# Edge rows placed in source order by plain scatters, and the edge sum of a four-layer graph network taken on TensorE without accumulating scatters

## What is computed

```python
def _L3_gnn_ref(x, edge_index, edge_attr, u, batch, W1, b1, W2, b2, Wa, ba, Wb, bb):
    row, col = (edge_index[0], edge_index[1])
    h = jnp.concatenate([x[col], edge_attr], axis=1)
    h = jax.nn.relu(h @ W1.T + b1)
    h = jax.nn.relu(h @ W2.T + b2)
    summed = jax.ops.segment_sum(h, row, num_segments=n)
    ...
    agg = summed / jnp.maximum(cnt, 1.0)[:, None]
    z = jnp.concatenate([x, agg, u[batch]], axis=1)
    z = jax.nn.relu(z @ Wa.T + ba)
    return z @ Wb.T + bb
```

## Time and profile before

| what | value |
|---|---|
| median of 3 runs | 4369.33 us (4359.36 to 4374.9) |
| the profiled execution | 4391.7 us, its span 4390.0 us |
| PE busy | 2941.5 us (67%) |
| DVE busy | 2594.5 us (59%) |
| POOL busy | 2417.1 us (55%) |
| ACT busy | 1475.1 us (34%) |
| TensorE's granted clock, mean | 0.728 of full speed |
| DMA | 338.20 MB, 77 GB/s on average |

### The profile page before, as it was taken

One profiled execution on the slowest core, in us unless ns is written; L12 is line 12 of the kernel. 1 busy time (PEld: TensorE's weight loads), 2 busy tenths in 40 slices (PEclk: granted clock), 3 DMA queues, 4 the chain that ended last, 5 costly groups with the idle time before them and its releaser, 6 DMA issues. The chain is left out here.

```text
span 4390.0 us, 76379 instructions
## 1 busy us (share of the span) xinstructions
PE 2941.5 (67%) x16134; PEld 2027.4 (46%) x16135; DVE 2594.5 (59%) x9305; ACT 1475.1 (34%) x3181; POOL 2417.1 (55%) x1836
## 2 busy tenths in 40 slices
PE   1636666666666666656567785887878878778762
PEld 0324544444444454443232332666656666666541
DVE  6148888888888887776954443444344443444422
ACT  0124444444444444443010000443333333333320
POOL 0056666666666666550000000588888888888881
PEclk9955555555555555556778876888988989899876
DMA  1353333333333333782603230455555555555543
GB/s 43 100 125 98 97 95 102 97 97 108 90 97 97 106 98 89 86 103 98 169 25 86 71 93 4 47 54 54 53 54 53 54 54 53 54 54 53 54 43 74
DMA packets 654307, 338.20 MB, mean 77 GB/s; under 512 B 437168, under 2 KB 614627, under 8 KB 653284
## 3 DMA queue, kind: packets, MB, share of 16 engines
q0 software_dynamic: 148736, 86.57, 20.5%
q1 hardware_dynamic: 487814, 143.62, 15.5%
q10 hardware_dynamic: 17568, 106.20, 6.0%
HBM read 158.05 MB, written 202.84 MB: 82 GB/s over the span
## 5 line engine op out<-in xcount | busy, mean ns | idle before, releaser
L1847 POOL DMA_INDIRECT sums<-el_rows,el_idx x816 | 1269.2, 1555 | 782.2 <-DVE el_rows L2061 533.9
L828 POOL DMA_INDIRECT at_hs<-table,at_rec_s x976 | 1140.3, 1168 | 614.9 <-DVE at_hw L1122 310.3
L966 PE MATMUL near_ps<-at_pair_hot,at_src_low_hot 128*128 128x425 f16 x976 | 507.4, 520 | 580.1 <-ACT at_count_s L864 319.8
L864 ACT CAST at_count_s<-near_ps 128x400 f16<-128x400 f32 x976 | 481.9, 494 | 987.5 <-PE near_ps L966 446.0
L2059 DVE CAST el_idx<-el_place 128x4 uint32<-128x4 f32 x204 | 35.3, 173 | 840.6 <-DMA sums<-el_rows,el_idx 791.8
L938 PEld LDWEIGHTS sums_ps<-at_hw,at_hit 128*128 128x128 f32 x1952 | 472.9, 334 | 36.3 <-issue 31.7
L966 PEld LDWEIGHTS near_ps<-at_pair_hot,at_src_low_hot 128*128 128x128 f16 x976 | 135.4, 139 | 722.8 <-ACT at_count_s L864 397.9
L938 PE MATMUL sums_ps<-at_hw,at_hit 128*128 128x66 f32 x1952 | 442.2, 408 | 8.7 <-DVE acc L1012 8.7
L1409 PE MATMUL sum_total<-chunk,sum_parts 128*128 128x512 f16 (+1 forms) x700 | 264.2, 391 | 119.9 <-DVE chunk L1511 98.3
L1004 DVE TENSOR_SCALAR at_pair_hot<-iota_wide,at_rec_s 128x400 f16<-128x400 f16 x976 | 324.7, 335 | 0.0
L1995 ACT ACTIVATE el_h<-el_h_ps,el_valid 128x128 f32<-128x128 f32 x816 | 232.6, 368 | 239.3 <-PE el_h_ps L1909 175.8
(11 more groups left out here) (339 smaller groups left out, 5095.2 us busy)
## 6 DMA issues: line engine op xcount, KB each, us to landing
slots<-at_count_s ACTq DMA_DIRECT2D x122, 850.0 KB
chunk<-slots SPq DMA_DIRECT2D x480, 100.0 KB
el_rec<-attr SPq DMA_DIRECT2D x816, 32.0 KB
attr<-in_edge_attr SPq DMA_DIRECT2D x19, 1248.0 KB
at_rec_s<-meta SPq DMA_DIRECT2D x992, 3.5 KB
at_hs<-table,at_rec_s POOLq DMA_INDIRECT x976
el_pair<-meta SPq DMA_DIRECT2D x816, 1.0 KB
sums<-el_rows,el_idx POOLq DMA_INDIRECT x816
```

The costliest lines, as they stand in the source:

```text
L828: pool.indirect_dma_start(hs[:, s, u, :], None, k.table, bass.IndirectOffsetOnAxis(rec[:, s, u, 0:1].bitcast(U32), 0)).then_inc(gathered[s ...
L864: a.copy(count[:, (n.o + d) % 2, i, 0:AW], near[:, (n.o + d) % 2, 0:AW]).then_inc(count_ready, 1)
L966: pe.matmul(near[:, s, 0:SW], low_hot[:, s, i, :], pair_hot[:, s, i, :], start=False, stop=True, skip_group_check=(i > 0)).then_inc(near_r ...
L1847: pool.indirect_dma_start(k.sums_flat[a], bass.IndirectOffsetOnAxis(idx[:, j, a:a + 1], 0), rows[:, j, a, :], None, compute_op=ALU.add).th ...
```

## The change

- A new stage `edge_places` counts, for each of the 25 tiles of source nodes, the edges before each edge (VectorE's scans, sums over partitions on TensorE), and writes for every edge its end node, its source and its place in the order of source tiles (`edge_ends`). It also makes the visits of the edge loop, now for tiles of source nodes; the second pass of `schedule` goes.
- All 782 columns of edge rows (64 features, the end node and the source: 66 words) are scattered to their places in `edge_rows`, one indirect DMA of 128 rows per column. 244 of them (two a step) are in attention, behind the step's 8 gathers; the other 538 are in blocks of 17 (the last has 11) in the stages from ln0 to edge_tables: 1 in ln0, 6 in the first neighbour sum, 1 in the degree layer, 1 in ln1, 5 in each further neighbour sum, 1 in each linear layer, 1 in ln2, and 4 (62 columns) in edge_tables. Three buffers hold a piece or a block. The copy into `attr` and the zeroing go.
- The edge loop, again 102 visits of 8 tiles, loads edge rows of one tile of source nodes, and POOL gathers the end nodes' rows of x beside them (816 gathers). TensorE turns both together, one product with K = 128 takes the place of y and the mask, and the sum over sources is a product with a one-hot matrix of the source within its tile (`hot`). VectorE adds the result to `edge_sum` in SBUF, at a tile read from a table.
- `node_update` takes `edge_sum` as it is. The tables y in edge_tables go; x is written to HBM there (`node_rows`).

```diff
+PIECE = 2
+PARTS = 3
+BLOCK = 17
+
+NB3 = -(-(EC + NT) // (3 * B)) * 3
+LATER = EC - PIECE * NB0
+SIZES = [min(BLOCK, LATER - b) for b in range(0, LATER, BLOCK)]
...
+def edge_places(nc, k):
+
+    with Stage(nc) as c:
...
+            pe.wait_ge(count_ready, 1)
+            pe.matmul(before[:, 0:NT], k.below[:], count[:], start=True, stop=True)
+            pe.matmul(column[:, 0:NT], k.ones_f[:], count[:], start=True, stop=True).then_inc(counted, 1)
+            for t in range(NT):
+                pe.wait_ge(value_ready, t + 1)
+                for i in range(2):
+                    m = pe.matmul(place[:, i, 0:W], k.ident[:], value[:, t % 3, i * W:(i + 1) * W], start=(t == 0),
+                                  stop=(t == NT - 1))
+                m.then_inc(value_added, 1)
...
+            for t in range(NT):
+                v.tensor_scalar(mask[:, t], k.tile_h[:], float(t), None, ALU.is_equal).then_inc(run_ready, 1)
+                if t:
+                    dve.wait_ge(run_ready, 2 * t)
+                    v.tensor_tensor_scan(run[:, t - 1], mask[:, t - 1], none[:], 0.0, ALU.add, ALU.add).then_inc(run_ready, 1)
...
+            for t in range(NT):
+                if t >= 3:
+                    dve.wait_ge(value_added, t - 2)
+                v.scalar_tensor_tensor(value[:, t % 3], run[:, t], base[:, t:t + 1], mask[:, t], ALU.add, ALU.mult
+                                       ).then_inc(value_ready, 1)
...
+            dve.wait_ge(value_added, NT)
+            for i in range(2):
+                v.tensor_copy(k.row_ends[:, i * W:(i + 1) * W, 2].bitcast(U32), place[:, i, 0:W]).then_inc(place_ready, 1)
...
+            def piece(n, d):
+
+                s = (n.o + d) % PARTS
+                if n.after(PARTS - d):
+                    sp.wait_ge(part_placed[s], n.thirds(d) * (16 * PIECE))
+                    sp.sem_inc(passed, 1)
+                sp.dma_start(part[:, s, :, 0:D], features[:, bass.ds(n(PIECE, d * PIECE), PIECE), :]).then_inc(part_loaded[s], 16)
+                sp.dma_start(part[:, s, :, D:ER + 1], row_ends[:, bass.ds(n(PIECE, d * PIECE), PIECE), :]
+                             ).then_inc(part_loaded[s], 16)
...
-            for a in range(NACC):
-                for i in range(8):
-                    sp.dma_start(k.sums_flat[a].rearrange("(p r) h -> p (r h)", p=P)[:, i * ZW:(i + 1) * ZW],
-                                 k.zero[:]).then_inc(sums_zeroed, 16)
...
+                s = n.o % PARTS
+                pool.wait_ge(part_loaded[s], n.thirds(0) * 32 + 32)
+                pool.sem_inc(passed, 1)
+                for i in range(PIECE):
+                    pool.indirect_dma_start(k.edges, bass.IndirectOffsetOnAxis(part[:, s, i, ER:ER + 1].bitcast(U32), 0),
+                                            part[:, s, i, 0:ER], None).then_inc(part_placed[s], 16)
...
+def place_blocks(nc, k, pool, blocks):
+
+    for b in blocks:
+        s = b % PARTS
+        pool.wait_ge(k.block_loaded[s], 32 * (b // PARTS + 1))
+        for i in range(SIZES[b]):
+            pool.indirect_dma_start(k.edges, bass.IndirectOffsetOnAxis(k.block_rows[:, s, i, ER:ER + 1].bitcast(U32), 0),
+                                    k.block_rows[:, s, i, 0:ER], None).then_inc(k.block_placed[s], 16)
...
+                for b, after in zip(blocks, due_after):
+                    if after == i < DC - 1:
+                        load_block(nc, k, act, b + PARTS)
...
+                    pool.wait_ge(loaded[s], it * (16 * B) + 16 * B)
                     pool.sem_inc(passed, 1)
-                    for a in range(NACC):
-                        if not (first and j == 0):
-
-                            pool.wait_ge(added[a], it * 64 + 16 * j)
-                            pool.sem_inc(passed, 1)
-                        pool.indirect_dma_start(k.sums_flat[a], bass.IndirectOffsetOnAxis(idx[:, j, a:a + 1], 0),
-                                                rows[:, j, a, :], None, compute_op=ALU.add).then_inc(added[a], 16)
-            body(0, True)
+                    for u in range(B):
+                        pool.indirect_dma_start(edge[:, s, u, 0:D], None, k.nodes,
+                                                bass.IndirectOffsetOnAxis(edge[:, s, u, 2 * D:2 * D + 1].bitcast(U32), 0)
+                                                ).then_inc(gathered[s][u // 4], 16)
...
+                    t = pe.transpose(z_ps[:, j % 2, u * P:(u + 1) * P], edge[:, s, 4 * h + u, 0:2 * D], k.ident[:])
+                t.then_inc(turned, 1)
...
+                pe.matmul(h1_ps[:, j % 2, :], k.w1[:], z_t[:, j % 2, :], start=True, stop=True).then_inc(h1_ready, 1)
...
+                v.tensor_tensor(hot[:, j % 2], own[:, s, 4 * h:4 * h + 4].unsqueeze(2).to_broadcast([P, 4, P]),
+                                k.iota_row[:].unsqueeze(1).to_broadcast([P, 4, P]), ALU.is_equal).then_inc(hot_ready, 1)
...
+            def adds(q, j, m, first):
+                tiles = tiles_of(m, j % 2)
                 dve.wait_ge(sum_ready, q + 1)
-                dve.wait_ge(join_ready, n1)
-                if done is not None:
-                    for a in range(NACC):
-                        dve.wait_ge(added[a], done)
-                ch(v.tensor_copy(idx[:, j], place[:, s, 4 * h:4 * h + 4]))
-                ch.wait()
-                v.tensor_copy(rows[:, j].rearrange("p u h -> p (u h)"), sum_ps[:, j % 2, :]).then_inc(rows_ready, 1)
+                for u in range(4):
+                    to = k.part[:, bass.ds(tiles[u], 1), :].rearrange("p t h -> p (t h)")
+                    if u or not first:
+                        dve.wait_ge(added, q * 4 + u)
+                    v.tensor_tensor(to, to, sum_ps[:, j % 2, u * P:(u + 1) * P], ALU.add).then_inc(added, 1)
...
+            layernorm(nc, k, "ln0", x_t=k.x_t, ahead=range(AHEAD), blocks=blocks(1))
+            neighbour_sum(nc, k, 0, range(DC), blocks(6))
+            degree_layer(nc, k, blocks(1))
+            layernorm(nc, k, "ln1", x_t=k.x_t, blocks=blocks(1))
             keep(nc, k)
...
+                neighbour_sum(nc, k, i + 1, range(DC) if i % 2 else range(DC - 1, -1, -1), blocks(5))
+                linear_layer(nc, k, i, blocks(1))
+            layernorm(nc, k, "ln2", x_t=k.x_t, blocks=blocks(1))
...
+            edge_tables(nc, k, blocks(len(SIZES)))
             edge_loop(nc, k)
-        node_update(nc, k)
```

More of the change, by code:

```diff
@@ L1454, in _ @@
                 pe.sem_inc(skipped, 1)
+        @block.gpsimd
+        def _(pool):
+            place_blocks(nc, k, pool, blocks)
+        due_after = [-(-(i + 1) * DC // len(blocks)) - 1 for i in range(len(blocks))]
         @block.scalar
@@ L1480, in _ @@
             act.wait_ge(copied, DC)
+            for b, after in zip(blocks, due_after):
+                if after == DC - 1:
+                    load_block(nc, k, act, b + PARTS)
         @block.vector
@@ L2162, in _ @@
             step(v.reciprocal(share[:], share[:]))
-            dve.wait_ge(loaded, 16 * NACC)
-            for a in range(1, NACC):
-                step(v.tensor_tensor(part[:, 0], part[:, 0], part[:, a], ALU.add))
-            v.tensor_tensor(part[:, 0], part[:, 0], share[:].unsqueeze(2).to_broadcast([P, NT, H]),
+            v.tensor_tensor(mean[:], k.part[:, 0:NT], share[:].unsqueeze(2).to_broadcast([P, NT, H]),
                             ALU.mult).then_inc(mean_ready, 1)
@@ L2255, in gnn_stack_kernel @@
                 group_records(nc, k)
+                edge_places(nc, k)
             with ExitStack() as c1:
```

586 lines of the change are left out of this document (283 added, 303 removed).

## The result

| | median | runs |
|---|---|---|
| kernel before | 4372.11 us | 4 (4359.36 to 4379.41) |
| changed kernel | 5139.16 us | 4 (5129.51 to 5172.04) |

The ratio is 1.177 (95% interval 1.171 to 1.183). The prediction said 4105 us, 4020 to 4290; the kernel became 767 us slower, 1034 us above the forecast. The profiled execution has a span of 5127.8 us.

The account below looks back on a forecast made before the run. POOL's queue was taken to bound the edge loop, with its 816 accumulating scatters. The terms 116 + 48 + 98 - 495 - 31 gave -264 us, a median of 4105 us, range 4020 to 4290.

Parts of the forecast that it names:

- edge_places: New stage with nothing beside it: 123 us, less 7 for schedule's tile pass, so +116, between +90 and +160.
- ln0 to ln2: Middle stages before edge_tables: scatters add +25 in the three later neighbour sums and +22 in the layer norms.
- rival of slow scatters: Attention and middle stages: plain scatters cost 1.86 us like accumulating ones, so the change is slower, 4461 us; chance 0.09.
- gathers at 1.46 in the loop: Edge loop: gathers cost attention's 1.46 us, so 1191 us in place of 1050, total 4246 us; chance 0.14.
- 0.13 given to slower: Whole kernel: chance 0.13 that the change makes it slower, against 0.86 for faster.
- 816 x 1.25: Edge loop: POOL's 816 gathers at 1.25 us take 1020 us, with extras 1065, against 1560: -495.
- close behind: Edge loop: TensorE, 4.7 us for four tiles against POOL's 5.1, is what is late next.
- 14.65: Attention: ten indirect DMAs and a second wait make a step 14.65 us against 14.26, POOL the bound, +48.
- 2.5 us a step to spare: Attention: POOL's 310 us wait for VectorE's at_hw was read as some 2.5 us a step of spare time.
- sign given for a step above 15.4 us: Attention: such a step would show the prediction wrong, the new wait or SP's loads being late, not POOL's work.
- 102 x 1.35 = 138 in 151 us, nothing: First neighbour sum: 102 scatters at 1.35 us take 138 us, hidden in the stage's 151 us, adding nothing.
- TensorE at its low level: Edge loop: waits for gathers hold TensorE at 1.2 GHz, a round 8.3 us, total 4746 us; chance 0.04.

Follow-up runs that it names:

- changed_third: The changed kernel as it is, run again in a later comparison whose kernel before took 4203 us: 4322 us, ratio 1.029.
- old_att_paced: The kernel before with a 0.20 us POOL fill behind each gather of attention: 4213 us, beside 4207 us for the unchanged kernel.
- old_att_paced_again: The kernel before with a 0.20 us POOL fill behind each gather of attention, in another comparison: ratio 1.0026 to the unchanged kernel.
- second and third comparison: Two sets of kernels run on the same chip, each with the kernel before among them; it took 4207 us in the second, 4345 us in the third.
- loop_paced: The changed kernel with a POOL scratch fill (0.46 us) behind each gather of the edge loop: 4967 us, kernel before 4383 us.
- both_paced: The changed kernel with POOL fills of 0.20 us behind each indirect DMA of attention and 0.46 us behind each edge loop gather: 4890 us, ratio 1.126.
- changed_again: The changed kernel as it is, run again in a comparison whose kernel before took 4345 us: 5045 us, ratio 1.162.
- adjust_psum: The changed kernel with the neighbour sums' count adjusting split into two VectorE instructions of one SBUF input each, through PSUM: 5212 us, ratio 1.201.

## Why the prediction was wrong

The step that failed is the one that turns work into time: in each large stage the prediction took the busiest engine's work as the time of the stage, and let waits and other engines' work hide behind it. The runs showed three things in its place. In the edge loop TensorE's completions came late and no engine's work set the pace (-79 in place of -495). In attention POOL's time to spare was itself mostly such a wait (+346 in place of +48). In the stages from ln0 to ln2 VectorE's and POOL's times added up (+352 in place of +47). The terms, beside the recorded run (slow steps) and changed_third (none):

| term | predicted | recorded | without slow steps |
|---|---|---|---|
| edge_places | +116 | +91 | +88 |
| attention | +48 | +346 | +196 |
| ln0 to ln2 | +47 | +352 | +292 |
| edge_tables | +51 | +59 | +59 |
| edge loop, from SP's first load | -495 | -79 | -489 |
| node_update | -31 | -35 | -34 |

The third column is worked out against the trace of old_att_paced (4213 us), the only one of the kernel before without slow steps, so its attention has the fills (the unchanged kernel of that comparison took 4207, so they made no difference). The columns sum to +734 and +112 where the totals differ by 738 (spans) and 109. Even without slow steps the sum is off by 376 us and has the wrong sign: the term for ln0 to ln2 is off by 245 us and that for attention by 148.

**The price of one indirect DMA: right where VectorE leaves POOL alone.** Plain scatters 0.97 us at the median with 0.30 behind, gathers 0.97 in the loop and 1.14 in attention. The rival of slow scatters (1.86 us) and the one of gathers at 1.46 in the loop are both refuted. The result is on the slow side for neither's reason, so the 0.13 given to slower rested on mechanisms that didn't occur.

**edge_places, edge_tables, node_update: right** within 28 us, the first at the low end of its bounds (90 to 160): the scans cost 1.78 us against 1.8, and the 25 values with their products took 37 us in place of 50.

**The edge loop: right as work, wrong as a forecast.** "816 x 1.25" and 1066 us is what it takes when nothing is late (then TensorE is busy 3.9 us a round, by 798.75 / 204). The failing step is that TensorE was put "close behind" POOL by its busy time alone, 4.7 of 5.1 us. Between two products of a round lies ScalarE, so a completion that comes 4 us late costs the round 4 us, and nothing in 5.1 us can take that up. I looked for contention on POOL's side (VectorE's inputs), not for what POOL's pace does to others. The trace had shown it: in attention of the kernel before ScalarE waits 165 of 1000 us (600 to 1600) for "remote", which I didn't follow up, and SP's move has a maximum of 731 ns:

```profile
L864 ACT CAST at_count_s<-near_ps 128x400 f16<-128x400 f32 x563 | 277.8, 493 | 505.1 <-PE near_ps L966 206.2 <-remote 164.9 <-issue 125.4
...
L784 SPq MOVE at_rec_s<-meta x992: 2/29/731, 205.5 to 1943.7; - x199
```
In the loop of the kernel before ScalarE waits for TensorE by name and for "issue" only the earlier trace rows. Whoever puts attention's pace into the loop has to ask what else attention has.

**Attention: the new step right, the old one misread.** "14.65" was the sum, and 14.44 is what it takes without slow steps. But the 14.26 us of the kernel before were not its work: without slow steps it takes 12.82 (old_att_paced), and 12.61 in the changed kernel without its scatters. So most of POOL's 2.5 us a step to spare was a wait caused by the late completions and no reserve: without slow steps POOL waits 67 us in all for at_hw (old_att_paced), 0.5 us a step, where it waited 310. Of the two scatters' 2.6 us a step 1.83 show: +196. With slow steps there are more of them beside ten indirect DMAs a step than beside eight (385 against 243): 17.12 us, +346. The new wait and SP's loads cost nothing, as predicted, as far as the variants without slow steps show. The sign given for a step above 15.4 us came true, but its reading, that the new wait or SP's loads would be late, isn't what the runs show.

**The stages behind attention: the wrong law.** "102 x 1.35 = 138 in 151 us, nothing" took the slower of the two engines' times; while VectorE's instructions with two SBUF inputs follow each other, the times add. The rule was known, and applied in the loop, where it hardly matters (a gather's mean there is 0.968 us, its median 0.944). L1511 in the kernel before would have told, 32 instructions in 17.55 us, without a gap:

```profile
2320.34 17.55 DVE L1511 SCALAR_TENSOR_TENSOR chunk<-chunk,minus_past 128x400 f16<-128x400 f16 x32 [23.42 <-DMA chunk<-slots]
```

These stages cost 292 us in place of 47, of which leaving the adjusting out gives back 207 (709 to 502 us in the four neighbour sums); slow steps add 60.

**TensorE at its low level (0.04):** the clock is 0.78 in the loop with slow steps and 0.96 without. It doesn't set the pace: at 0.78 TensorE is busy 972 / 204 = 4.8 us of a round of 7.3. That the lower clock follows from TensorE's waits is likely by this, but no run tests it.

**The noise.** The prediction took 0.3%, 13 us, as what a measurement tells from no change. Runs of one kernel lay up to 55 us apart within a comparison (old_att_paced_again), and between comparisons the kernel before went from 4203 to 4383 us.

**What stays open:** what else differs between comparisons with and without slow steps. The same chip showed both (second and third comparison), so it isn't the chip alone. Which part of an indirect DMA's issue makes completions late, and by what way, is open too, and so is whether the time between two DMAs counts or the number of them in flight, since a pause changes both.

## What to carry to other kernels

A pace of POOL at which the other engines' completions come late can show up in one stage of the kernel before the change: look for waits with no named releaser and for register steps of SP of 0.7 us before moving that pace elsewhere, and try a pause between indirect DMAs (0.33 us helped here, 0.08 didn't). Beside back-to-back VectorE instructions with two SBUF inputs, add POOL's time to VectorE's; don't take the larger. And a stage's time before is its work only if its waits are explained: a reserve read from an unexplained wait may not be there.

## What the runs showed of the hardware

- With slow steps about, indirect DMAs of 128 rows 1.25 or 1.33 us apart make SP's register steps take 0.70 or 1.40 us, and TensorE's and VectorE's completions come late (VectorE's 1.69 us; TensorE's 3.9 us in the stretch shown, over 1 us in 95 of 204 rounds of the recorded loop); at 1.58 us apart they don't (2 slow steps in the loop, no late round), nor do accumulating scatters 1.86 us apart (9 slow steps, none of 204 products L1898 late). Where slow steps are absent, 1.25 us apart does no harm either (changed_third: none of 204 late).
- In one neighbour sum this lasted the whole run of scatters. SP issued ten loads in the 41 us from 2890.5 to POOL's last scatter (2930.9 to 2931.9), thirteen in the 13 us behind it, and ScalarE waited 49 us for TensorE (12 us in the kernel before), until POOL paused; the name behind the arrow is wrong again:

```profile
2890.47 54.70 SPq L1456 DMA_DIRECT2D chunk<-slots  x23
...
2939.00 0.59 ACT L1622 COPY agg_t<-sum_total 128x512 f32<-128x512 f32 x1 [49.06 <-DMA at_hs<-table,at_rec_s]
```

- An added pause made a kernel faster: 816 x 0.33 us more work on POOL, 172 us less in all (loop_paced against the recorded run), and a loop of 1320 in place of 1440 us within one comparison (both_paced, changed_again).
- POOL's scatter isn't let in between VectorE instructions with two SBUF inputs that follow each other: 49.37 us for one scatter, and never over 2.00 us where the same arithmetic goes through PSUM (adjust_psum).
- A plain scatter costs what a gather does, 0.97 + 0.30 us for 128 rows of 264 B; an accumulating one of 128 rows of 512 B costs 0.58 us more. Which of the two, the addition or the longer row, costs it isn't separated.
